# A vision tower on one core: experts 2 to 7 computed on sorted tiles of 128 slots, and the attention stage before them rearranged

## The chip, the cores and the metric

The kernel runs on one core of a Trainium2 chip. The time is that of the device, in microseconds (us); before the change it is 227.14, the median of three runs (226.74 to 228.03). One execution was profiled, and its trace is what is read here.

## The reference

64 images give 36 patches each; a patch embedding, a window attention and a pooled attention with a class row make five rows of 256 numbers per image, and `cls_tok` is put in front, so that there are 6 tokens of 256 for each of 64 images. What follows is an attention over the 6 tokens with a residual, and a mixture of eight experts with a residual:

```python
h = jnp.concatenate([jnp.broadcast_to(cls_tok, (h.shape[0], 1, h.shape[2])), h], axis=1)
h = h + _L0_attn_ref(_layernorm(h, axis=-1), ...)          # 16 heads, causal, ALiBi
h = h + _L0_ffn_ref(_layernorm(h, axis=-1), ...)
# _L0_ffn_ref: E = 8 experts, D = 256, F = 512, two of them for each token
router_probs = jax.nn.softmax(x_flat @ gate_w, axis=-1)
top_k_probs, top_k_idx = jax.lax.top_k(router_probs, TOP_K)      # TOP_K = 2
top_k_probs = top_k_probs / jnp.sum(top_k_probs, axis=-1, keepdims=True)
gate_up = jnp.einsum('nd,edh->enh', x_flat, gate_up_w)
hidden = jax.nn.silu(gate_up[..., :F]) * gate_up[..., F:]
expert_out = jnp.einsum('enf,efd->end', hidden, down_w)
output = jnp.sum(sel * top_k_probs[:, :, None], axis=1)          # sel: the two chosen experts' rows
```

Token 0 is the same for every image up to here (causal attention lets it see only itself), so only 5 x 64 + 1 = 321 rows differ.

## The kernel before, in words

All five engines run instruction streams written out by hand, and every dependence is a counted semaphore; nothing is scheduled by a tool. The order in the source is the order on the engine.

Precision: a product of two fp32 matrices that matters for the routing is made from float32r halves. A tile has a high part (`HI`, a cast, on ScalarE) and a low part (`LO`, the tile minus its high part, on VectorE or GpSimd), and three matmuls (`PRODUCTS`) are summed. So all weights of `gate_up` and `down` pass through `weights_hi` and `weights_lo` before they are used. Other matmuls are plain fp32; the profile has two MATMUL records for each of those.

The stages, in the order of time:

1. The patch convolution (L419, L434), turns (L443), keys and values of the window attention (L496), up to 78.5 us. VectorE makes the scores and weights of the window attention beside it.
2. From 78.5 to 129.5 us: the weighted values are summed by TensorE (`tail_agg`, L539: 18 matmuls against the identity for each of two row tiles), projected (`tail_proj`), added to the window means on VectorE (`local_out`), normalised and turned (`tail_pool`), the pooled scores of the class row (L686), its softmax, and then the projections and softmax of the attention over 6 tokens in three blocks (`att_scores`, `att_weights`), the weighted values (L357 on GpSimd and VectorE), their turns (L634), the output projection (L643), three layer norms (`mid`) and the router (L657). `keep_clock` (L664) are matmuls whose result nobody reads.
3. From 129.5 us: the experts. Every expert is applied to all 322 columns (`NCOL`) of the turned rows `ms`. `gate_up(q, n)` (L744) makes one of four chunks of 128 hidden units, gate in one bank and up in another, with 12 matmuls of 322 columns (two halves, two pieces of the 256 inputs, three products); ScalarE applies Silu, VectorE multiplies, and both split the result into `hids`. `down(s, e)` (L757) makes three banks of 128 rows, 12 matmuls each, and `accumulate` (L1523) adds them to `acc` with the router's weight, which is zero for the experts not chosen. Two experts' weights (1536 KB each) are held in `raw`, loaded by SP, and the next pair's are loaded as the splits of these are done.
4. The rows are stored by SP and ScalarE's queue; the class row goes from one partition of `acc` to its 64 places.

## Time and profile before

| | |
|---|---|
| median of three runs | 227.14 us |
| the profiled execution's own time | 228.78 us |
| its span in the trace | 227.0 us |
| TensorE, matmuls | 207.6 us busy, 1368 records |
| VectorE | 155.6 us busy, 363 |
| ScalarE | 101.6 us busy, 225 |
| GpSimd | 79.5 us busy, 91 |
| mean granted TensorE clock | 0.985 |
| moved by DMA | 23.01 MB, 101 GB/s over the span |

PE is TensorE, PEld its weight loads, DVE VectorE, ACT ScalarE, POOL GpSimd, SP the engine that issues DMAs; SPq is SP's queue. A timeline row gives the start, the length, engine, line, operation, tiles and count of merged records, and in brackets the idle time before it and who ended it. The length of a merged row holds the last record's way through the array too, so the pace is read from the start of one row to the start of the next.

### The profile page before, as it was taken

Reading aid. Unit: us, or ns where it says so; the run is one execution under the profiler, and the core shown is the slowest. Engines: PE = TensorE matmul, PEld = TensorE weight load, DVE = VectorE, ACT = ScalarE, POOL = GpSimd, SP = SyncE. Lnnn points to the kernel's source line nnn. Section 1 sums busy time; section 2 is a strip of 40 time slices with the busy share of each in tenths; the row PEclk is TensorE's granted clock in tenths of the full one; section 3 lists DMA queues with packets and bytes.
Section 4 is the critical chain, followed back from the end, with each engine's and each line's share of the span. In section 5 each row is a group of like instructions: output and inputs, shape, how many; then the busy total and the mean of one; then the engine's idle time right before and its main releaser. Section 6 shows DMA issues by size and latency. Waiting matters only on the chain.

```text
span 227.0 us, 4002 instructions
## 1 busy us (share of the span) xinstructions
PE 207.6 (91%) x1368; PEld 192.4 (85%) x1368; DVE 155.6 (69%) x363; ACT 101.6 (45%) x225; POOL 79.5 (35%) x91
## 2 busy tenths in 40 slices
PE   2999989999999988789587989999999999999983
PEld 2898969898987878477386889999999999999983
DVE  2565981929696767577987599576957785858541
ACT  3754581835354516334122177383718371717030
POOL 0037093555428302270643315233423332333200
PEclk9999999999999999969889999999999999999999
DMA  6999910002910000000000005172533253400004
GB/s 222 360 394 373 339 52 3 3 0 54 423 80 1 3 0 0 0 3 0 1 0 0 3 0 206 76 277 53 225 128 149 43 234 97 180 0 3 0 0 69
DMA packets 4890, 23.01 MB, mean 101 GB/s; under 512 B 694, under 2 KB 2444, under 8 KB 3724
## 3 DMA queue, kind: packets, MB, share of 16 engines
q1 hardware_dynamic: 3960, 21.26, 26.3%
q10 hardware_dynamic: 916, 1.58, 2.0%
q8 instruction: 8, 0.13, 0.2%
q14 instruction: 6, 0.05, 0.1%
HBM read 22.44 MB, written 0.39 MB: 101 GB/s over the span
## 4 chain that ended last, share of the span: by engine, by line
PE 82%; DVE 8%; ACT 3%; DMA 2%; issue 2%; POOL 0%; SPq 0%; DVEq 0%
PE bank L744 26%; PE bank L757 15%; PE bank L419 11%; PE bank L496 9%; PE bank L539 4%; PE bank L434 3%; DMA raw<-conv_w 2%; PE bank L443 2%; PE bank L634 2%; PE bank L618 2%; PE bank L643 1%; PE bank L476 1%; DVE stats L1162 1%; PE bank L657 1%; PE bank L694 1%
## 5 line engine op out<-in xcount | busy, mean ns | idle before, releaser
L744 PE MATMUL bank<-split 128*128 128x322 f32 x384 | 59.2, 314 | 0.6 <-DVE vprod L1531 0.6
L744 PEld LDWEIGHTS bank<-split 128*128 128x128 f32 x384 | 57.6, 188 | 0.9 <-issue 0.9
L1147 POOL TENSOR_TENSOR split<-raw,split 128x256 fp32r<-128x256 f32 x32 | 29.0, 906 | 56.7 <-DVE split L1484 56.7
L757 PE MATMUL bank<-split 128*128 128x256 f32 x288 | 36.0, 283 | 0.6 <-DVE split L1537 0.6
L757 PEld LDWEIGHTS bank<-split 128*128 128x128 f32 x288 | 35.4, 192 | 0.8 <-DVE split L1537 0.8
L419 PE MATMUL bank<-split 128*128 128x256 f32 (+1 forms) x225 | 28.2, 284 | 1.0 <-DVE split L1259 1.0
L419 PEld LDWEIGHTS bank<-split 128*128 128x128 f32 (+1 forms) x225 | 27.5, 191 | 1.5 <-DVE split L1259 1.4
L1044 POOL TENSOR_TENSOR rstd<-veps,mhalf 128x1 f32<-128x1 f32 (+2 forms) x17 | 14.2, 838 | 38.5 <-DVE veps L1169 38.4
L496 PE MATMUL bank<-split 128*128 128x512 f32 x108 | 26.9, 399 | 0.0
L1011 ACT ACTIVATE vprod<-bank 128x322 f32<-128x322 f32 x32 | 13.9, 436 | 24.8 <-PE bank L744 24.7
L1531 DVE TENSOR_TENSOR vprod<-bank,vprod 128x322 f32<-128x322 f32 x32 | 15.7, 491 | 12.0 <-PE bank L744 8.5
L496 PEld LDWEIGHTS bank<-split 128*128 128x128 f32 x108 | 19.8, 188 | 3.9
L1479 DVE TENSOR_TENSOR split<-raw,split 128x512 fp32r<-128x512 f32 x29 | 20.7, 712 | 2.3 <-ACT split L881 2.2
L1019 ACT CAST split<-vprod 128x322 fp32r<-128x322 f32 x32 | 14.8, 463 | 16.4 <-DVE vprod L1531 16.3
L881 ACT CAST split<-raw 128x512 fp32r<-128x512 f32 x32 | 19.5, 613 | 2.5 <-DMA raw<-ffn_w 2.5
L1523 DVE SCALAR_TENSOR_TENSOR pe_rows<-bank,wgt,pe_rows 128x256 f32<-128x256 f32 x24 | 11.2, 479 | 11.1 <-PE bank L757 11.1
L1162 DVE BATCH_NORM_STATS2 stats<-pe_rows 128x6 f32<-128x256 f32 x24 | 9.0, 418 | 12.5 <-ACT pe_rows L794 12.3
L1058 POOL TENSOR_TENSOR window<-window,pe_rows 128x256 f32<-128x256 f32 x14 | 13.7, 982 | 9.0 <-ACT pe_rows L794 8.4
L1537 DVE TENSOR_TENSOR split<-vprod,split 128x322 fp32r<-128x322 f32 x32 | 15.9, 497 | 1.4 <-ACT split L1019 1.4
L855 ACT ACTIVATE kv_rows<-bank,rstd 128x512 f32<-128x512 f32 x18 | 12.0, 690 | 8.5 <-PE bank L496 8.5
L794 ACT COPY pe_rows<-bank 128x256 f32<-128x256 f32 x18 | 6.5, 374 | 18.7 <-PE bank L419 17.0
L434 PE MATMUL bank<-split 128*128 128x256 f32 (+1 forms) x45 | 9.1, 385 | 5.1 <-ACT split L808 5.1
(161 smaller groups left out, 276.2 us busy)
## 6 DMA issues: line engine op xcount, KB each, us to landing
raw<-ffn_w SPq DMA_DIRECT2D x8, 1536.0 KB, 6.5
raw<-xa SPq DMA_DIRECT2D x5, 768.0 KB
tok<-tok_w SPq DMA_DIRECT2D x1, 1536.0 KB, 12.4
tok<-tok_w SPq DMA_DIRECT2D x1, 776.0 KB, 6.4
raw<-xa ACTq DMA_DIRECT2D x1, 576.0 KB, 5.1
raw<-xb SPq DMA_DIRECT2D x6, 96.0 KB
att<-att_w SPq DMA_DIRECT2D x1, 488.0 KB, 13.9
raw<-conv_w SPq DMA_DIRECT2D x1, 384.0 KB, 5.7
```

Of the source, the lines that this page charges most:

```text
L419: mm = pe.matmul(bank[b][:, 0:C], xs[0:n, g % 2, px, a:a + P], cws[0:n, pw, k, :], start=(k == 0 and m == 0), stop=(k == len(KCH) - 1 and ...
L434: mm = pe.matmul(bank[j][:, 0:C], xs[0:n, 0, px, a:a + P], cws[0:n, pw, k, :], start=(k == 0 and m == 0), stop=(k == len(KCH) - 1 and m == 2))
L496: mm = pe.matmul(bank[b][:, :], lns[:, g % 2, px, a:a + P], wkvs[:, pw, aw:aw + 2 * C], start=(c == 0 and m == 0), stop=(c == CC - 1 and m ...
L744: mm = pe.matmul(bank[b][:, 0:NCOL], aws[:, q, pw, a:a + P], ms[:, px, c, FIRST:ROWS], start=(c == 0 and m == 0), stop=(c == CC - 1 and m ...
L757: mm = pe.matmul(bank[b][:, 0:C], hids[:, px, s * FQ + q, a:a + P], bws[:, s, pw, q * C:(q + 1) * C], start=(q == 0 and m == 0), stop=(q = ...
L881: act.copy(aws[:, q, HI, :], a_raw[:, slot, q, :]).then_inc(a_hi, 1)
L1019: act.copy(hids[:, HI, s * FQ + q, FIRST:ROWS], hidf[:, q % 2, :]).then_inc(hid_hi, 1)
L1044: pool.tensor_tensor(rstd[0:parts, k, 0:n], veps[0:parts, k, 0:n], mhalf[0:parts, 0:n], ALU.pow).then_inc(rstd_done, 1)
L1147: pool.tensor_tensor(bws[:, s, LO, q * C:(q + 1) * C], b_raw[:, s, q, :], bws[:, s, HI, q * C:(q + 1) * C].bitcast(F32), ALU.subtract).the ...
L1479: dve.tensor_tensor(aws[:, q, LO, :], a_raw[:, slot, q, :], aws[:, q, HI, :].bitcast(F32), ALU.subtract).then_inc(a_split, 1)
L1531: dve.tensor_tensor(hidf[:, q % 2, :], bank[5 + q % 2][:, 0:NCOL], sg[:, q % 2, :], ALU.mult).then_inc(hid_done, 1)
L1537: dve.tensor_tensor(hids[:, LO, s * FQ + q, FIRST:ROWS], hidf[:, q % 2, :], hids[:, HI, s * FQ + q, FIRST:ROWS].bitcast(F32), ALU.subtract ...
```

## The change

It has two parts. Both are in the diff, which is cut to its core.

**Experts.** Experts 0 and 1 (`DENSE`) stay as they were. For experts 2 to 7 the rows that chose one are counted and given slots, each expert from a multiple of 128 on; with 321 rows, 2 picks and 6 experts that needs at most 10 tiles of 128 slots (`SLOT_TILES`), and 10 are always computed. VectorE works out the slots (steps 11 to 29 of `route_step`), GpSimd scatters each row with its number and its weight to `expert_rows` in DRAM with six indirect DMAs, whose unused slots were filled with zeros long before, from `zero_row`, by SP. SP reads the expert of each tile into a register (`value_load`) and loads its weights into rings of three (`a_ring`, `b_ring`), and the rows of a tile into one of four row buffers (`xr`). For a tile, TensorE turns the rows, makes gate and up as 12 matmuls of 512 columns with the rows as the stationary operand, turns the product, makes the down product as 4 plain fp32 matmuls and puts the result back to its rows with 6 matmuls against a 0/1 matrix `back`, which GpSimd makes; these sums stand in three banks over all ten tiles. Expert 1's down products come at the end (`late_down`), and three VectorE additions close the sums.

**Before the experts.** The window attention's weighted values are summed partly on VectorE and GpSimd; the biases and residuals go through TensorE into the same bank; the pooled rows are no longer normalised and turned a second time, their norm is folded into the weights (`gwvc`, `uc`) and scores; the class row's softmax runs on 128 partitions instead of 8; two of the three layer norms in each set are applied by ScalarE straight from the bank; the second attention block's products move from GpSimd to VectorE, and blocks are taken in the order 0, 2, 1.

```diff
+DENSE = 2
+SPARSE = E - DENSE
+SLOT_TILES = (PICKS * NTOK - SPARSE) // P + SPARSE
+RING = 3
+ROW_RING = 4
...
+            sp.wait_ge(zero_ready, 1)
+            sp.dma_start(expert_rows[0:SLOTS, :].rearrange("(s p) n -> p s n", p=P), spread(zero_row[:, :], 1, SLOT_TILES)).then_inc(zeroed, 16)
...
-            with sp.Fori(1, E // 2) as pair:
...
+            sp.wait_ge(route_step, ROUTED)
+            expert = [sp.value_load(tile_expert[0:1, s:s + 1], min_val=DENSE, max_val=E - 1) for s in range(RING)]
+            tile_a(0, expert[0])
+            tile_b(0, expert[0])
+            tile_a(1, expert[1])
+            expert += [sp.value_load(tile_expert[0:1, s:s + 1], min_val=DENSE, max_val=E - 1) for s in range(RING, SLOT_TILES)]
+            sp.wait_ge(scattered, PICKS * RT * 16)
+            for s in range(ROW_RING):
+                tile_rows(sp, s)
...
+            def class_values_mean():
+                wait_free(pe, 7, "gwv_mean")
+                pe.wait_ge(tok_rest_in, 16)
+                for m in range(CC):
+                    for c in range(CC):
+                        pe.matmul(bank[7][:, C + m:C + m + 1], gwv[:, c, m * P:(m + 1) * P], w_tok("gkv_b")[:, c:c + 1], ...)
+                pe.wait_ge(gwv_scaled, 1)
+                for c in range(CC):
+                    mm = pe.matmul(bank[7][:, 0:C], mean_w[:, :], gwvc[:, c, :], start=(c == 0), stop=(c == CC - 1))
...
+            def second_aggregate():
...
+                for n in (*range(GT), *range(2 * GT, NW)):
+                    if n % GT == 0:
+                        pe.wait_ge(vprod_step, VSTEPS + (4 if n else 3))
+                    for c in range(CC):
+                        mm = pe.matmul(bank[c][:, 0:P], vprod[:, n, c * P:(c + 1) * P], ident, start=(n == 0), stop=(n == NW - 1))
...
+            def tile_gate_up(s):
+                pe.wait_ge(rows_split, s + 1)
+                for half in range(2):
...
+                    for c in range(CC):
+                        piece = half * CC + c
+                        pe.wait_ge(tile_a_split, FQ * s + piece + 1)
+                        for m, (px, pw) in enumerate(PRODUCTS):
+                            mm = pe.matmul(bank[half][:, :], xst[:, s % 2, px, c * P:(c + 1) * P], aws[:, piece, pw, :], ...)
+                        mm.then_inc(tile_a_used, 1)
...
+            for s in range(SLOT_TILES):
+                tile_gate_up(s)
+                if s + 1 < SLOT_TILES:
+                    rows_turn(s + 1)
+                if s:
+                    tile_out(s - 1)
+                if s > 1:
+                    give_back(s - 2)
+                if s + 1 == SLOT_TILES:
+                    late_down(2)
+                hidden_turn(s)
+            give_back(SLOT_TILES - 2)
+            late_down(0)
+            tile_out(SLOT_TILES - 1)
+            late_down(1)
+            give_back(SLOT_TILES - 1)
...
+            for j in range(RT):
+                for i in range(PICKS):
+                    scatter(i, j)
+            way_back(0)
+            for q in range(FQ):
+                down_lo(1, q)
...
+            for s in range(SLOT_TILES):
+                if s + 1 < SLOT_TILES:
+                    tile_weights_lo(s + 1, 0)
+                tile_product(s)
+                if s + 1 < SLOT_TILES:
+                    rows_lo(s + 1)
+                    for piece in range(1, FQ):
+                        tile_weights_lo(s + 1, piece)
+                if s:
+                    out_lo(s - 1)
...
+            for i, (j, _) in enumerate(OUT_BANKS):
+                dve.wait_ge(sums_full, i + 1)
+                dve.wait_ge(acc_done, 2 * RT + i + 1)
+                dve.tensor_tensor(acc[:, j, :], acc[:, j, :], bank[SUM_BANK[j]][:, 0:C], ALU.add).then_inc(result_done, 1)
```

TensorE's experts before, one expert of the loop, its last chunk of `gate_up` and its `down` (L744 is `gate_up`, L757 `down`):

```order
L744 MATMUL bank<-split 128x322 x12
L751 ISA
L757 MATMUL bank<-split 128x256 x12
L751 REGISTER_ALU
L757 MATMUL bank<-split 128x256 x12
L751 REGISTER_ALU
L757 MATMUL bank<-split 128x256 x12
```

TensorE now, from expert 0 on and through the first three tiles (L954 dense `gate_up`, L964 dense `down`, L977 the counts, L986 `rows_turn`, L1001 `tile_gate_up`, L1010 `hidden_turn`, L1019 `tile_out`, L1031 `give_back`):

```order
L977 MATMUL bank<-mask,ones 128x6
L954 MATMUL bank<-split 128x322 x60
L964 MATMUL bank<-split 128x256 x36
L954 MATMUL bank<-split 128x322 x24
L986 MATMUL bank<-con,window 128x128 x2
L1001 MATMUL bank<-split 128x512 x12
L986 MATMUL bank<-con,window 128x128 x2
L1010 MATMUL bank<-con,kv_rows 128x128 x4
L1001 MATMUL bank<-split 128x512 x12
L986 MATMUL bank<-con,window 128x128 x2
L1019 MATMUL bank<-kv_rows,loT 128x256 x4
L1010 MATMUL bank<-con,kv_rows 128x128 x4
```

The tile loop has taken the place of six of eight experts; expert 1's `down` is no longer behind its `gate_up`.

VectorE now, in the routing (L1998 is `hidden`, the product of a dense chunk, L2061 the low part of expert 1's weights, L2003 the low part of the hidden rows, the others slot arithmetic):

```order
L2041 TENSOR_TENSOR pick_eq<-pick_eq,swgt 128x18
L2043 TENSOR_REDUCE pe_rows<-pick_eq 128x3
L2045 TENSOR_TENSOR pe_rows<-swsum,pe_rows 128x3
L1998 TENSOR_TENSOR vprod<-bank,vprod 128x322
L2047 TENSOR_TENSOR kv_rows<-tile_no,first_tile 128x60
L2049 TENSOR_REDUCE tile_sum<-kv_rows 128x10
L2051 TENSOR_SCALAR tile_expert<-tile_sum 128x10
L2061 TENSOR_TENSOR split<-raw,split 128x512
L1998 TENSOR_TENSOR vprod<-bank,vprod 128x322
```

Before, the router's steps stood together ahead of the first product; now they stand between the products of expert 0, and the first low part of expert 1's weights is behind all of them.

SP now, from the last of the first three register loads to the rows of the first tiles (`window` holds `xr`, `kv_rows` and `raw` the rings); of the seven loads at L521 the last is shown:

```order
L517 TENSOR_LOAD tile_expert
L517 ISA x2
L507 ISA
L507 DMA kv_rows<-ffn_w 128x2048
L513 ISA
L513 DMA kv_rows<-ffn_w 128x1024
L507 ISA
L507 DMA raw<-ffn_w 128x2048
...
L521 TENSOR_LOAD tile_expert
L521 ISA x2
L429 DMA window<-expert_rows 128x258 x4
```

The rows of tile 0 are the fourth thing SP does after the routing, behind ten register loads and three weight loads.

## Rows read from the trace of the kernel before

**Rows 1.** The page: busy time by engine, and the chain by line.
```profile
PE 207.6 (91%) x1368; PEld 192.4 (85%) x1368; DVE 155.6 (69%) x363; ACT 101.6 (45%) x225; POOL 79.5 (35%) x91
...
PE bank L744 26%; PE bank L757 15%; PE bank L419 11%; PE bank L496 9%; PE bank L539 4%; PE bank L434 3%; DMA raw<-conv_w 2%; PE bank L443 2%; PE bank L634 2%; PE bank L618 2%; PE bank L643 1%; PE bank L476 1%; DVE stats L1162 1%; PE bank L657 1%; PE bank L694 1%
```

**Rows 2.** Windows: stretch, length, busy and count by engine, clock, DMA share, GB/s.
```profile
78.50:96.00 17.50, 14.85 (x104) 12.80 (x103) 10.73 (x26) 6.79 (x21) 2.67 (x5) 1.00 0.00 0
96.00:113.00 17.00, 13.43 (x51) 9.97 (x50) 13.90 (x30) 5.10 (x17) 8.65 (x11) 0.86 0.01 1
...
133.90:222.00 88.10, 87.44 (x637) 87.27 (x638) 62.38 (x144) 42.94 (x93) 27.50 (x30) 1.00 0.29 108
```

**Rows 3.** Timeline of PE, the experts: start, length, what, idle before.
```profile
141.22 4.48 PE L757 MATMUL bank<-split 128*128 128x256 f32 x36
145.54 7.36 PE L744 MATMUL bank<-split 128*128 128x322 f32 x48
152.73 4.48 PE L757 MATMUL bank<-split 128*128 128x256 f32 x36
...
220.01 3.49 PE L757 MATMUL bank<-split 128*128 128x256 f32 x27 [0.61 <-DVE split L1537]
```

**Rows 4.** Timeline of PE, earlier stages.
```profile
22.05 0.82 PE L443 MATMUL bank<-con,pe_rows 128*128 128x128 f32 x6
22.62 5.63 PE L419 MATMUL bank<-split 128*128 128x256 f32 x45
...
28.67 4.34 PE L496 MATMUL bank<-split 128*128 128x512 f32 x18
33.97 5.64 PE L419 MATMUL bank<-split 128*128 128x256 f32 x45 [0.97 <-DVE split L1259]
...
101.40 1.89 PE L694 MATMUL bank<-poolT,tok 128*128 128x256 f32 x8
```

**Rows 5.** Groups by line and shape: busy us, mean ns, idle before.
```profile
L1479 DVE TENSOR_TENSOR split<-raw,split 128x512 fp32r<-128x512 f32 x29 | 20.7, 712 | 2.3 <-ACT split L881 2.2
...
L881 ACT CAST split<-raw 128x512 fp32r<-128x512 f32 x32 | 19.5, 613 | 2.5 <-DMA raw<-ffn_w 2.5
...
L855 ACT ACTIVATE kv_rows<-bank,rstd 128x512 f32<-128x512 f32 x18 | 12.0, 690 | 8.5 <-PE bank L496 8.5
...
L1523 DVE SCALAR_TENSOR_TENSOR pe_rows<-bank,wgt,pe_rows 128x256 f32<-128x256 f32 x24 | 11.2, 479 | 11.1 <-PE bank L757 11.1
...
L1408 DVE TENSOR_TENSOR split<-bank,split 128x256 fp32r<-128x256 f32 x3 | 1.3, 421 | 1.2 <-ACT split L968 1.2
...
L1440 DVE TENSOR_TENSOR kv_rows<-bank,kv_rows 128x512 f32<-128x512 f32 x1 | 0.7, 693 | 1.2 <-PE bank L702 1.2
```

**Rows 6.** Timeline: marks of the attention stage and of the routing.
```profile
85.53 4.26 PE L539 MATMUL bank<-con,vprod 128*128 128x128 f32 x36 [0.24 <-DVE vprod L348]
...
95.48 1.03 PE L686 MATMUL bank<-poolT,u 128*8 128x256 f32 x4 [0.90 <-ACT poolT L798]
...
110.69 0.23 DVE L1387 TENSOR_TENSOR kv_rows<-kv_rows,r 128x72 f32<-128x72 f32 x1
...
129.65 0.18 DVE L1488 COPY lg<-bank 128x24 f32<-128x24 f32 x1 [0.92 <-PE bank L657]
...
133.21 0.18 DVE L1515 TENSOR_TENSOR wgt<-rtop,rrec 128x24 f32<-128x24 f32 x1
```

**Rows 7.** Timeline: GpSimd and VectorE at the same time.
```profile
107.35 1.54 POOL L366 TENSOR_TENSOR vprod<-kv_rows 128x640 f32<-128x640 f32 x1 [5.25 <-ACT kv_rows L951]
...
107.44 1.53 DVE L1374 TENSOR_TENSOR kv_rows<-kv_rows,m 128x72 f32<-128x72 f32 x1
```

**Rows 8.** The DMA view: GB/s by slice of 5.7 us; issues, KB each, us to landing.
```profile
GB/s 222 360 394 373 339 52 3 3 0 54 423 80 1 3 0 0 0 3 0 1 0 0 3 0 206 76 277 53 225 128 149 43 234 97 180 0 3 0 0 69
...
raw<-ffn_w SPq DMA_DIRECT2D x8, 1536.0 KB, 6.5
...
out<-pe_rows ACTq DMA_DIRECT2D x3, 64.0 KB, 2.8
```

More of the change, by code:

```diff
@@ L700, in _ @@
[L700 to L708 removed]
+            second_aggregate()
+            local_rows(1)
@@ L1010, in chunk @@
                 act.wait_ge(gate_ready, n + 1)
-                act.activation(sg[:, q % 2, :], bank[q % 2][:, 0:NCOL], ACT.Silu).then_inc(silu_done, 1)
-                if not (last and s == 1 and q + AHEAD_A >= FQ):
-                    nxt = q + AHEAD_A >= FQ
-                    slot = (s + nxt) % 2
-                    loads = 16 * (pair + 1 + (s + nxt) // 2)
-                    weights_hi(slot, (q + AHEAD_A) % FQ, loads if (q + AHEAD_A) % FQ == 0 else None)
-                act.wait_ge(hid_done, n + 1)
@@ L1019, in chunk @@
-                act.copy(hids[:, HI, s * FQ + q, FIRST:ROWS], hidf[:, q % 2, :]).then_inc(hid_hi, 1)
-            with act.Fori(0, E // 2 - 1) as pair:
-                for s in range(2):
-                    for q in range(FQ):
-                        chunk(2 * pair + s, s, q, pair, False)
-            for s in range(2):
-                for q in range(FQ):
-                    chunk(E - 2 + s, s, q, E // 2 - 1, True)
+                if n >= 2:
+                    act.wait_ge(hid_done, n - 1)
@@ new lines, in scatter, with way_back @@
+            def scatter(i, j):
+                pool.indirect_dma_start(expert_rows, bass.IndirectOffsetOnAxis(ap=dest_row[:, i, j:j + 1], axis=0),
+                                        xrow[:, j, i, :], None).then_inc(scattered, 16)
+            def way_back(s):
+                wait_tile_in(pool, rows_in, s)
+                pool.wait_ge(*((given, s - 1) if s >= 2 else (down_done, RT)))
+                pool.tensor_scalar(back[:, s % 2, :], token_row[:, :], xr[:, s % ROW_RING, ROW_TOKEN:ROW_TOKEN + 1], None,
+                                   ALU.is_equal).then_inc(back_done, 1)
@@ L1540, in expert_pair @@
-            def expert_pair(pair, last):
-                for s in range(2):
-                    e = 2 * pair + s
-                    for q in range(2, FQ):
-                        chunk(e, s, q, pair, last)
-                    if not (last and s == 1):
-                        for q in range(2):
-                            chunk(e + 1, 1 - s, q, pair + s, last)
-                    accumulate(e)
-            chunk(0, 0, 0, 0, False)
-            chunk(0, 0, 1, 0, False)
-            with dve.Fori(0, E // 2 - 1) as pair:
-                expert_pair(pair, False)
```

1250 lines of the change are left out of this document (842 added, 408 removed).

## The prediction

> **What bounds the kernel now.** First the page's busy line and the chain by line: TensorE is busy 207.6 of 227.0 us, and the two expert lines L744 and L757 make 41% of the chain, more than any other pair [rows 1]. Then the windows: from 133.9 to 222.0 TensorE is busy 87.4 of 88.1 us at full clock while VectorE has 62 and ScalarE 43, so the experts cost what their matmuls cost. From 78.5 to 113 it is different: TensorE idles 2.7 and 3.6 us, the clock granted from 96 to 113 falls to 0.86, and VectorE is as busy as TensorE, 13.9 of 17.0 us [rows 2]. There a chain through all engines decides. So the change is priced twice: by matmuls in the experts, by the chain before them. I measure both from one mark, the copy of the router's logits on VectorE: 129.65 [rows 6]. Behind it lie 227.0 - 129.65 = 97.4 us.
>
> **Paces of TensorE.** From starts of merged rows: a split matmul of 322 columns takes (152.73 - 145.54)/48 = 0.150 us, of 256 columns (145.54 - 141.22)/36 = 0.120 [rows 3]; of 512 columns 4.34/18 = 0.241; a turn of 128x128 (22.62 - 22.05)/6 = 0.095; four plain fp32 matmuls of 256 columns 1.89 [rows 4].
>
> **Experts, the work.** Six dense experts go: each 48 x 0.150 + 36 x 0.120 = 11.5 us, together 69. A tile costs 12 x 0.241 = 2.89 for gate and up, 2 x 0.095 = 0.19 to turn the rows, 1.89 for down, 6 x 0.120 = 0.72 to give back, 4 x 0.095 = 0.38 to turn the product: 6.07, ten tiles 60.7. The counts add about 0.5. On TensorE alone the change is worth 69 - 61.2 = 7.8 us. A sparse count does not show in it, since ten tiles are always run.
>
> **Experts, is a tile TensorE's?** VectorE has per tile four low parts at 0.71, a product of 512 columns 0.69, the rows' low part 0.42 and the output's 0.48: 4.4 us. ScalarE has four high parts at 0.61 and four others of at most 0.69: 5.2 [rows 5]. Both are under 6.07. In order: with t from the start of gate and up, its four pieces are used at 0.7, 1.4, 2.2, 2.9. ScalarE refills them at 1.4, 2.8, 4.2, 4.8, its Silu lying between the first two and the rows' high part before the third. VectorE makes the product by 3.7 and the last low part by about 6.2, against a need at 8.2 (6.07 + 3 x 0.72). The turn of the product, at 5.7, finds it ready since 3.7. Each hand-over has 2 us to spare, so the period is TensorE's. Weights: 1.57 MB and 0.13 MB of rows per tile are 280 GB/s at this period; slices of the trace show 394 and 423 [rows 8]. Each load is issued more than one period ahead. I cost DMA at nothing; its cover is that distance.
>
> **Experts, the start**, in us after the mark. TensorE does the first chunk to 1.8, counts to 2.6, and three more chunks to 8.0. VectorE's router steps go at 0.2 to 0.35 each; before, the twelve took from 129.65 to 133.4 [rows 6]. Now 23 more stand between the first products. At about 0.21 each and 0.49 per product, the slots are out at 7.5, the tile numbers at 8.6 and the first low part of expert 1's weights at 9.3. The fifth chunk waits for that: 1.3 us idle. Then chunks to 12.9, expert 0's down (36 x 0.12 = 4.3) to 17.2, two chunks to 20.8, the turn of the first rows to 21.0, and their high and low parts (0.37 and 0.42, with hand-overs): tile 0 starts at 22.0. Tiles 0 and 1 are uneven, since ScalarE must also cast four pieces of expert 1's down weights in tile 0, and its delay reaches down product, Silu and the next rows; by the same bookkeeping tile 2 starts at 31.8. Seven periods later it is 74.3. The last tile, without a row turn and with one late down group of 12 x 0.12 = 1.44, takes 7.3. The tail is 0.72 + 1.44 + 1.89 + 1.44 + 0.72 = 6.2. Last matmul: 87.8. From the last matmul to the end the trace has 227.0 - 223.5 = 3.5 us [rows 3], and the last step, one VectorE operation on 256 columns and a store, is of the same kind. That gives 91.3, against 97.4: **6.1 us gained**.
>
> **What the start hides.** Six indirect scatters, a read-back, and ten register loads are in no row. One scatter costs GpSimd no less than a short queue entry and no more than the 2.8 us a 64 KB store takes from issue to landing [rows 8]; I take 1.1, nearer to the GpSimd operations of its size, so issue ends at 14.2 and data has landed at 16.5. A register load lies between 0 and 2.8 too; I take 0.7, so SP has its three at 10.7, the three weight loads out at 12, the other seven at 17. Rows then land at about 20, against a need at 20.8. If both cost next to nothing nothing is won, since the chunks cover them. At the upper end of either, SP or GpSimd is done 12 to 15 us later. I add 0.5 for this. The zeros are issued right behind the last patch load, in the first quarter of the span, long before the scatters wait for them.
>
> **The stage before.** It starts worse. `class_values_mean` puts four one-column and two plain matmuls, 1.75 us, where TensorE stood idle for 0.97 [rows 4]: +0.8. VectorE gains two value products and two sums there and delays the class keys by 0.5. The second aggregate, which ran 85.5 to 89.8 as 18 matmuls [rows 6], starts at 86.0 behind a VectorE sum and has 12: it ends at 88.9. From there a chain is shortened link by link. The projection lands on its bias, and the copied rows are ready at 90.7 against 92.1. The pooled norm's apply, its turn and two affine copies are gone, so the pooled scores come at 91.5 against 95.5. The softmax of the class row and the projections behind it keep this lead, and the block-0 weights are done at 106.4 against 110.9 [rows 6]. Then GpSimd's three value products, a turn, the projection, and for the last row tile a context turn of 9 matmuls at 114.3, the projection at 117.9, statistics at 118.8, GpSimd's root behind three splits and two copies at 120.3, the norm, turn and split, and the router. The logits come at 123.6 instead of 129.65: **6.0 us gained**, by durations of rows 4 and 5. No row shows `negative_mean`; I take 0.3 to 0.5 for it, in the chain once.
>
> Where VectorE and GpSimd meet, the trace has this: a VectorE operation on 72 columns took 1.53 us, exactly beside a GpSimd operation of 1.54 [rows 7]. By the Trainium skill (SBUF — State Buffer, Who interferes with whom) a VectorE instruction with two SBUF inputs and a GpSimd one that reads SBUF take turns at a shared port, and the second blocks until the first ends; the trace agrees. By that rule, `way_back` blocks VectorE once in a tile, for up to its 0.7 us or so, and 4.4 becomes 5.1, which still changes nothing; in the routing it speaks against the change, and is part of a rival.
>
> **The sum.** 228.8 - 6.1 - 6.0 + 0.5 = 217.2 for an execution under the profiler. The median of the runs shown is 227.14 where this one took 228.8, so 1.6 less: 215.6. I round to 216, since two hand-overs per stage will be longer than booked.
>
> **Rivals.**
> 1. *The tiles wait for their rows.* Scatters or register loads at 1.5 to 2.5 us, or VectorE's four low parts and GpSimd's scatters held up by each other as in rows 7, move tile 0 by 2 to 6 us. For it: all of this stands in one line from the slots at 7.5 to the need at 20.8, with under 1 us to spare. Against it: 12 us of chunks lie over it. 216 + 2 to 6 = 218 to 222.
> 2. *The stage before gains little.* VectorE and GpSimd were busy there, products were moved to VectorE, and ScalarE gets the norms. Each link may give back half: +3 to +5, so 219 to 221.
> 3. *Slower: the tile loop is paced by something else.* If weights come as the eight loads did, 6.5 us for 1536 KB, one at a time, a tile of 1.7 MB takes 7.2 us, and the loop 10 us more: 226. It turns to slower from 7.3 us a tile, (227 - 216)/10 above 6.07 + 0.1. At 8 us, with scattered rows and weights in each other's way, it is 234. Against it: the loads overlap, and the slices at 394 and 423 GB/s need 4 us per tile.
> 4. *More is gained.* The clock no longer falls to 0.86, and TensorE's idle time there shrinks: 212 to 214.
>
> **Chances.** Forecast 214 to 218: 0.5. Rival 1: 0.22. Rival 2: 0.12. Rival 3: 0.06, of which 0.04 slower. Rival 4: 0.1. About 0.5%, 1.1 us, is what a measurement of this kernel tells from no change. Faster 0.94, same 0.02, slower 0.04. The range leaves out the far half of rival 1 and all of rival 3: 212.5 to 221.5.
>
> **What would show it.** Right: `tile_gate_up` rows of 12 matmuls starting 6.0 to 6.2 us apart from tile 2 on; the logits' copy at 122.5 to 125; the first tile 21 to 23 us after it; TensorE idle once for about 1 us before the fifth chunk. Wrong: VectorE or ScalarE busy over 90% in the tile loop with TensorE idle in each period (rival 3 in another form), TensorE waiting for a DMA of `expert_rows` before the first tile (rival 1), or the logits later than 126 (rival 2).

## The result and the profile after

The changed kernel takes 225.86 us (median of 20 runs, 224.51 to 229.19) beside 227.24 us before in the same series (226.19 to 229.47): a ratio of 0.9923, 95% interval 0.9896 to 0.9951. It is faster, by 0.8% and not by the 5% that were forecast; 225.86 lies 4.4 us above the upper end of the range. The profiled execution took 225.82 us, its span is 224.0 us. Here and below, medians and spreads are of all executions, while ratios leave out the few, of either kernel, that took over 1.5% longer than the fastest of the same kernel.

First the page of the kernel after, three lines of it: busy time, the clock by slice of 5.6 us, the chain by line.

```profile
PE 199.7 (89%) x1190; PEld 175.0 (78%) x1190; DVE 145.1 (65%) x338; ACT 114.4 (51%) x247; POOL 79.3 (35%) x103
...
PEclk9999999999999999999999999976999999999999
...
PE bank L1001 12%; PE bank L552 10%; PE bank L1019 7%; PE bank L629 6%; DMA window<-expert_rows 5%; DMA expert_rows<-pe_rows,dest_row 3%; PE bank L1031 3%; POOL expert_rows L1545 2%; DMA raw<-xb 2%; PE bank L853 2%; PE bank L964 2%; PE bank L1010 2%; DVE stats L1621 2%; DVE split L1738 2%; PE bank L862 2%
```

TensorE is busy 7.9 us less than in [rows 1], yet the span is only 3.0 us shorter; and the execution profiled before was 1.6 us above its median, where this one is at its own, so the medians are only 1.4 us apart. What is new on the chain are two transfers of `expert_rows` and GpSimd's scatters, 10% of it together; what is new in the clock are two slices at 0.7 and 0.6, from 145.6 to 156.8 us. The windows of [rows 2], after:

```profile
78.50:96.00 17.50, 15.90 (x89) 12.56 (x87) 13.09 (x38) 7.93 (x24) 7.14 (x9) 1.00 0.00 1
96.00:113.00 17.00, 13.68 (x72) 11.49 (x73) 13.23 (x36) 7.29 (x25) 6.53 (x12) 1.00 0.01 1
```

The clock does not fall between 96 and 113 in this execution (0.86 before). In the second profile of the same kernel, after_again below, it is 0.96 from 78 us to the mark. The mark, the copy of the router's logits, is at 125.07 where [rows 6] have 129.65: the stage before gained 4.6 us. But 98.9 us lie behind the mark, where there were 97.4: **the sorted tiles and the tail lost 1.5 us**. The timeline of TensorE in the kernel after, from the last two dense chunks to tile 3:

```profile
141.51 3.76 PE L954 MATMUL bank<-split 128*128 128x322 f32 x24
149.40 0.69 PE L986 MATMUL bank<-con,window 128*128 128x128 f32 x2 [4.14 <-DMA window<-expert_rows]
151.01 2.50 PE L1001 MATMUL bank<-split 128*128 128x512 f32 x5 [0.92 <-DVE split L2073]
...
157.07 3.23 PE L1001 MATMUL bank<-split 128*128 128x512 f32 x12
160.35 1.89 PE L1019 MATMUL bank<-kv_rows,loT 128*128 128x256 f32 x8
162.44 3.02 PE L1001 MATMUL bank<-split 128*128 128x512 f32 x12
...
168.30 3.01 PE L1001 MATMUL bank<-split 128*128 128x512 f32 x12
```

and the chain of waits of the same stretch, start and length:

```profile
132.72 1.22 POOL expert_rows L1545
...
139.74 7.47 DMA expert_rows<-pe_rows,dest_row
147.22 0.02 issue
147.24 2.12 DMA window<-expert_rows
...
151.01 4.80 PE bank L1001 x12
```

To be seen: TensorE stands still for 4.14 us until the read-back of the rows (`window<-expert_rows`) has come, and the read-back waited for the last scatter. That one was issued at 139.74, its GpSimd instruction was over at 140.9, and its data counted as landed at 147.2, 6.3 us later. Then the first tile's 12 matmuls take 4.80 us where later ones start the next group after 2.9. The window from 145 to 157, with columns as in [rows 2]:

```profile
145.00:157.00 12.00, 6.31 (x21) 4.42 (x20) 4.17 (x10) 4.18 (x10) 1.26 (x1) 0.72 0.71 249
```

TensorE had been idle for over 4 us, and the clock granted is 0.72 on the mean: some of these matmuls run at the lower of the two levels (1.2 and not 2.4 GHz). Last the end, all engines of the kernel after:

```profile
217.16 0.88 PE L1031 MATMUL bank<-split 128*128 128x256 f32 x6
...
217.76 1.07 DVE L2129 TENSOR_TENSOR pe_rows<-pe_rows,bank 128x256 f32<-128x256 f32 x3
218.20 0.64 SPq L535 DMA_DIRECT2D out<-pe_rows  x1
218.53 3.01 ACTq L437 DMA_DIRECT2D out<-pe_rows  x3
```

The last matmul ends at 218.04, the kernel 6.0 us later; before it was 3.5. L535 is the store of the class row from one partition to its 64 places. It is issued 5.8 us before the end. In the kernel before, the timeline of SP has it 5.75 us before the end (227.0), but 2.3 us before the last matmul was over:

```profile
221.25 0.62 SPq L402 DMA_DIRECT2D out<-pe_rows  x1
```

### The profile page after: what moved, and what is told of

It reads as the page before. It is cut to its first block, busy times and chain, and to the rows that moved or that the text cites. A ratio compares the mean times of both kernels' runs of the same rounds, so it can differ in the third digit from the quotient of the medians.

```text
span 224.0 us, 3577 instructions
## 1 busy us (share of the span) xinstructions
PE 199.7 (89%) x1190; PEld 175.0 (78%) x1190; DVE 145.1 (65%) x338; ACT 114.4 (51%) x247; POOL 79.3 (35%) x103
## 4 chain that ended last, share of the span: by engine, by line
PE 55%; DVE 18%; DMA 10%; issue 5%; POOL 3%; ACT 3%; SPq 2%; ACTq 0%; DVEq 0%
PE bank L1001 12%; PE bank L552 10%; PE bank L1019 7%; PE bank L629 6%; DMA window<-expert_rows 5%; DMA expert_rows<-pe_rows,dest_row 3%; PE bank L1031 3%; POOL expert_rows L1545 2%; DMA raw<-xb 2%; PE bank L853 2%; PE bank L964 2%; PE bank L1010 2%; DVE stats L1621 2%; DVE split L1738 2%; PE bank L862 2%
## 5 line engine op out<-in xcount | busy, mean ns | idle before, releaser
L1001 PE MATMUL bank<-split 128*128 128x512 f32 x120 | 32.1, 418 | 0.9 <-DVE split L2073 0.9
L1552 POOL TENSOR_SCALAR split<-token_row,window 128x384 fp32r<-128x384 f32 x10 | 13.4, 1344 | 46.2 <-PE bank L1031 37.7
L1001 PEld LDWEIGHTS bank<-split 128*128 128x128 f32 x120 | 23.0, 200 | 6.4 <-DVE split L2073 1.3
L552 PEld LDWEIGHTS bank<-split 128*128 128x128 f32 (+1 forms) x225 | 27.6, 191 | 0.4 <-DVE split L1740 0.2
L629 PE MATMUL bank<-split 128*128 128x512 f32 x108 | 26.4, 397 | 0.0
L1471 POOL TENSOR_TENSOR rstd<-veps,mhalf 128x1 f32<-128x1 f32 (+2 forms) x17 | 14.2, 838 | 25.9 <-DVE veps L1628 25.7
L629 PEld LDWEIGHTS bank<-split 128*128 128x128 f32 x108 | 19.8, 188 | 3.9
L954 PE MATMUL bank<-split 128*128 128x322 f32 x96 | 15.3, 316 | 0.3 <-DVE split L2061 0.3
L1371 ACT CAST split<-raw 128x512 fp32r<-128x512 f32 x24 | 14.3, 621 | 2.1 <-PE bank L1001 2.1
L954 PEld LDWEIGHTS bank<-split 128*128 128x128 f32 x96 | 14.4, 188 | 0.6 <-DVE split L2061 0.6
L2082 DVE TENSOR_TENSOR kv_rows<-bank,kv_rows 128x512 f32<-128x512 f32 x10 | 6.9, 692 | 9.5 <-PE bank L1001 6.9
L567 PEld LDWEIGHTS bank<-split 128*128 128x128 f32 (+1 forms) x45 | 8.2, 277 | 5.4 <-ACT split L1099 5.4
L2066 DVE TENSOR_TENSOR split<-kv_rows,split 128x512 fp32r<-128x512 f32 x16 | 10.4, 686 | 2.6 <-ACT split L1371 2.5
L1738 DVE TENSOR_TENSOR split<-raw,split 128x1536 fp32r<-128x1536 f32 x5 | 8.8, 1754 | 4.7 <-ACT split L1108 4.7
L1371 ACT CAST split<-kv_rows 128x512 fp32r<-128x512 f32 x16 | 9.5, 620 | 2.0 <-DMA kv_rows<-ffn_w 1.1
```

What stands on the lines that cost most here:

```text
L552: mm = pe.matmul(bank[b][:, 0:C], xs[0:n, g % 2, px, a:a + P], cws[0:n, pw, k, :], start=(k == 0 and m == 0), stop=(k == len(KCH) - 1 and ...
L567: mm = pe.matmul(bank[j][:, 0:C], xs[0:n, 0, px, a:a + P], cws[0:n, pw, k, :], start=(k == 0 and m == 0), stop=(k == len(KCH) - 1 and m == 2))
L629: mm = pe.matmul(bank[b][:, :], lns[:, g % 2, px, a:a + P], wkvs[:, pw, aw:aw + 2 * C], start=(c == 0 and m == 0), stop=(c == CC - 1 and m ...
L954: mm = pe.matmul(bank[b][:, 0:NCOL], aws[:, q, pw, a:a + P], ms[:, px, c, FIRST:ROWS], start=(c == 0 and m == 0), stop=(c == CC - 1 and m ...
L1001: mm = pe.matmul(bank[half][:, :], xst[:, s % 2, px, c * P:(c + 1) * P], aws[:, piece, pw, :], start=(c == 0 and m == 0), stop=(c == CC - ...
L1371: act.copy(aws[:, piece, HI, :].rearrange("p (q n) -> p q n", q=FQ), a_ring[ring(s)][:, :, piece * P:(piece + 1) * P]).then_inc(tile_a_hi, 1)
```

## Experiments

Each version ran four to six times, after_again twelve times. Theory A, after this reading: four terms of the forecast were too small, each at its own place. (1) The scatters' data lands late because the weights of the first tiles, 2.5 MB, are on the same DMA engines. (2) The pause lets the clock fall, which stretches tiles 0 and 1. (3) The class row's store, not the last matmul, sets the end. (4) In the stage before, something in the class row's chain. The rivals are in the expectations. Ratios are to the kernel before, run on the same chip.

**rows_first: the weights behind the rows.**

```diff
             tile_a(0, expert[0])
-            tile_b(0, expert[0])
-            tile_a(1, expert[1])
...
             for s in range(ROW_RING):
                 tile_rows(sp, s)
+            tile_a(1, expert[1])
+            tile_b(0, expert[0])
             tile_b(1, expert[1])
```

> SyncE issues only tile 0's gate-and-up weights before it waits for the scattered rows; the weights of tile 1 and the down weights of tiles 0 and 1 are issued behind the four row loads. Theory A (the scatters' data lands 6.3 us after the last scatter because 2.6 MB of weights are on the same DMA engines): it lands in 2.3 to 3 us, the row turn starts 3 to 3.5 us earlier, at about 146, and tile 0 starts with it; tile 1's weights are then about 1 us late, so the kernel takes 223 us. Rival B (6.3 us is the scatter's own): the row turn stays at 149, the weights come later still, and the kernel takes 226 to 228 us.

224.29 us (223.11 to 225.88), ratio 0.9885 (0.9808 to 0.9962). The timeline of SP, then of TensorE:

```profile
144.20 1.76 SPq L429 DMA_DIRECT2D window<-expert_rows  x4
...
146.28 0.44 PE L986 MATMUL bank<-con,window 128*128 128x128 f32 x2 [0.58 <-DMA window<-expert_rows]
147.64 3.07 PE L1001 MATMUL bank<-split 128*128 128x512 f32 x12 [0.92 <-DVE split L2073]
...
154.42 0.66 PE L1010 MATMUL bank<-con,kv_rows 128*128 128x128 f32 x4 [3.49 <-DVE kv_rows L2082]
154.84 4.59 PE L1001 MATMUL bank<-split 128*128 128x512 f32 x12
```

The last scatter's instruction ended at 141.36, so its data landed in 2.8 us, not 6.3, and TensorE waits 0.58 us for the rows, not 4.14. Theory A (1) holds. The price was larger than I wrote: the weights of tile 1, issued at 146.15, took 6.25 us, and TensorE waits 3.49 us in tile 0. The pause has moved, and the slow stretch with it: tile 0's 12 matmuls take 3.07 us, and it is now tile 1's, behind the pause, that take 4.59 (mean clock 0.79 from 152 to 160). That the total fell at all can't be told from the changed kernel by these intervals; the wait's two places can.

**no_scatter: the whole of the start.**

```diff
-            for j in range(RT):
-                for i in range(PICKS):
-                    scatter(i, j)
...
-            sp.wait_ge(scattered, PICKS * RT * 16)
+            sp.wait_ge(zeroed, 16)
```

> The six scatters are left out (the tiles then compute on zeros, so the output lacks experts 2 to 7); SyncE reads the rows back once the zeros and its ten register loads are done. Theory A (what was mis-sized at the start is the way of the rows, and the cold clock that follows from it): TensorE is idle under 1 us before tile 0, tile 0 starts 22 us after the copy of the logits, tile 2 at 32, and the kernel takes 220 to 221 us. Rival (VectorE's and ScalarE's order, or the register loads, would have held tile 0 up anyway): tile 2 starts 35 us or more after the mark, and the kernel takes 223 us or more.

220.96 us (219.87 to 222.68), ratio 0.9751 (0.9680 to 0.9822). Its mark is at 125.10:

```profile
145.86 0.44 PE L986 MATMUL bank<-con,window 128*128 128x128 f32 x2 [0.59 <-DMA window<-expert_rows]
147.22 3.02 PE L1001 MATMUL bank<-split 128*128 128x512 f32 x12 [0.92 <-DVE split L2070]
...
156.89 2.99 PE L1001 MATMUL bank<-split 128*128 128x512 f32 x12
```

Tile 0 starts 22.1 and tile 2 31.8 us after the mark, and the last matmul ends 86.9 after it. The forecast had 22.0, 31.8 and 87.8. So the rest of its start (routing, chunks, splits, register loads) adds up right; what failed in it is the way of the rows. Two smaller errors cancel in that sum: before the fifth chunk TensorE waits 0.3 us and not 1.3, and before the turn of the rows it waits 0.6 where nothing was booked.

**keep_clock: the pause filled with matmuls that nobody reads.**

```diff
             gate_up(3, FQ + 3)
+            pe.wait_ge(route_step, PLACED)
+            keep_clock(3, 8)
             rows_turn(0)
```

> Eight fp32 matmuls on 256 columns, whose result nobody reads, fill 3.8 of the 4.1 us for which TensorE waits for the rows; nothing else moves. If the low granted clock behind the pause is what stretches tile 0 (4.8 us of gate and up in place of 2.9), tile 0 takes 2.9 us and tile 2 starts 1.6 us earlier: 224.2 us. Rival (tile 0 is stretched by ScalarE's and VectorE's pieces, which come late for the same reason as the rows): tile 0 stays at 4 us or more and the kernel at 225.5 to 226 us.

224.45 us (223.61 to 227.69), ratio 0.9868 (0.9788 to 0.9948). The timeline of TensorE, and the window from 145 to 157:

```profile
151.42 3.04 PE L1001 MATMUL bank<-split 128*128 128x512 f32 x12 [0.92 <-DVE split L2075]
155.73 3.23 PE L1001 MATMUL bank<-split 128*128 128x512 f32 x12
161.10 3.02 PE L1001 MATMUL bank<-split 128*128 128x512 f32 x12
```

```profile
145.00:157.00 12.00, 9.86 (x49) 7.83 (x49) 6.26 (x13) 6.05 (x15) 1.74 (x2) 1.00 0.71 256
```

The idle time is filled but for 0.59 us. The clock is 1.00, tile 0 takes 3.04 us in place of 4.80, and tile 2 starts 9.7 us behind tile 0 in place of 11.4. So the fall costs 1.7 us, as (2) says. The rows come no sooner: tile 0 starts 25.6 us after the mark (125.82).

**early_down: the pause filled with work that is needed.** Two of expert 1's three down groups go before tile 0.

```diff
             gate_up(3, FQ + 3)
+            for i, (j, b) in enumerate(OUT_BANKS[:2]):
+                pe.wait_ge(acc_done, RT + i + 1)
+                down(1, j, b)
             rows_turn(0)
...
-                if s + 1 == SLOT_TILES:
-                    late_down(2)
...
-            late_down(0)
```

ScalarE's `down_hi(1, q)`, GpSimd's `down_lo(1, q)` and VectorE's `accumulate(1, 2)`, `accumulate(1, 0)` and `hidden_lo(7)` move with them, ahead of the rows.

> Two of the three late down groups of expert 1 (12 matmuls each, 1.44 us) move from behind the last tiles into the pause before tile 0; the down weights' high parts go to ScalarE's pauses at 135 to 140 us, their low parts on GpSimd ahead of the first way_back, and the last hidden chunk is split before the rows. Theory A (the pause and the cold clock are real costs that useful work can fill): 2.9 us less at the end and 1.6 us less in tiles 0 and 1: 221.5 us. Rival (the two groups run into the row turn, or the last tiles need them as cover for their hand-overs): 1.5 to 2.5 us less in all: 223.5 us.

220.80 us (219.99 to 221.71), ratio 0.9726 (0.9674 to 0.9778); the expectation of theory A was 221.5.

```profile
146.68 0.62 PE L964 MATMUL bank<-split 128*128 128x256 f32 x3 [0.36 <-DVE split L2002]
148.11 2.05 PE L964 MATMUL bank<-split 128*128 128x256 f32 x15 [0.81 <-DVE split L2002]
149.99 0.38 PE L986 MATMUL bank<-con,window 128*128 128x128 f32 x2
151.30 3.02 PE L1001 MATMUL bank<-split 128*128 128x512 f32 x12 [0.92 <-DVE split L2072]
```

The turn of the rows waits for nothing now, and tile 0 starts as late after the mark as in the changed kernel (25.9 us) with 2.9 us of work less behind it. What TensorE still waits for, 0.36 and 0.81 us, are the low parts of the last hidden chunk. The clock stays at 1.00. The last matmul ends 87.1 us after the mark (93.0 in the changed kernel).

**front_only: one part alone**, the new stage before with all eight experts dense, by the code of the kernel before.

```diff
-            for s in range(SLOT_TILES):
-                tile_gate_up(s)
...
+            with pe.Fori(0, E // 2 - 1) as pair:
+                expert_pair(pair, False)
+            expert_pair(E // 2 - 1, True)
```

> The new stage before with the eight dense experts of the kernel before. Theory A (the parts add, and the sorted tiles lose what they should have gained): the logits' copy comes at 125.1, as in the changed kernel, and 97.4 us follow as before: a span of 222.5 us and 224.3 us in all, 1.5 us less than the whole change. Rival B (the sorted tiles do gain on the same start, or the dense experts run longer behind the new stage): 226 us or more.

225.12 us (222.96 to 225.98), ratio 0.9878 (0.9823 to 0.9933). In the profiled execution the mark is at 124.64 and the span 221.2, so 96.6 us lie behind the mark. The timeline of TensorE and of the class row's store:

```profile
214.22 3.50 PE L940 MATMUL bank<-split 128*128 128x256 f32 x27 [0.61 <-DVE split L1837]
...
215.46 0.61 SPq L508 DMA_DIRECT2D out<-pe_rows  x1
```

The store is issued 2.3 us before the last matmul's end and 5.7 before the kernel's. By the traces theory A holds: the sorted tiles, as the change has them, cost 2.3 us behind the mark instead of gaining. But the execution profiled was the fastest of six, 2.2 us below their median, at a clock of 1.00 throughout, and the median lies between the two expectations. By the runs the intervals of the two ratios, 0.9878 and 0.9923, overlap; that the half beats the whole is likely, not shown.

**no_class_store and class_rows: what sets the end.** The first leaves the class row's store out, so its output lacks that row. The second makes the class row's sums in 64 partitions:

```diff
-            table(token_row[:, :], [[1, ROWS]], 0, 0)
+            table(token_row[:, 0:2 * P], [[1, 2 * P]], 0, 0)
+            pool.memset(token_row[:, 2 * P:2 * P + B], float(2 * P + B - 1)).then_inc(tables_done, 1)
+            table(token_row[:, 2 * P + B:], [[1, P - B]], 2 * P + B, 0)
...
+                act.copy(hids[:, n // FQ, HI * FQ + n % FQ, 0:FIRST], spread(hidf[:, n % FQ, 1], 1, FIRST))
...
-            sp.dma_start(out[:, 0, :].unsqueeze(0), spread(acc[B - 1:B, 2, :], 1, B)).then_inc(out_done, 16)
+            sp.dma_start(out[:, 0, :], acc[0:B, 2, :]).then_inc(out_done, 16)
```

(and the low part likewise, on VectorE).

> The store of the class row to its 64 places is left out, nothing else. Theory A (this store sets the end, since its sum now comes with the other sums): the last matmul is followed by 4.3 to 4.6 us in place of 6.0, 224.3 us. Rival B (the other stores, issued 0.3 to 0.7 us later, end at the same time): 5.7 us or more, 225.7 us.

> The class row's sums are made in 64 partitions instead of one: the 62 unused columns of the dense chunks get a copy of the class column (one more ScalarE and one more VectorE operation on 62 columns a chunk), the table of token numbers repeats the class row's number, and the store reads 64 partitions, one place each. Theory A (the store from one partition is the slow one): as without that store, 224.3 us. Rival B (the store is no slower than others, or 16 small operations cost as much in the dense chunks): 225.7 us or more.

Without the store: 224.67 us (222.43 to 227.37), ratio 0.9862 (0.9781 to 0.9942), and 4.15 us from the last matmul's end (216.35) to that of the span (220.5). With 64 partitions: 223.88 us (223.07 to 224.84), ratio 0.9823 (0.9772 to 0.9874), its end:

```profile
217.65 0.88 PE L1031 MATMUL bank<-split 128*128 128x256 f32 x6
...
218.69 0.52 SPq L535 DMA_DIRECT2D out<-pe_rows  x1
219.02 1.82 ACTq L437 DMA_DIRECT2D out<-pe_rows  x3
```

218.53 to 222.7 are 4.2 us. Both ways 1.8 us are gone, so what is slow is the reading of one partition for 64 places, not the 64 KB; why, no run shows. It slows its neighbours too: by the DMA view the 64 KB stores at the end land 3.6 to 3.7 us after their issue in the changed kernel (medians), and 2.0 to 2.1 us after it in these two. Theory A (3) holds. That the total of class_rows fell by more than 1.8 us is within the intervals.

**combo, combo_class, combo_turn.** combo is early_down with expert 0's third down group behind the last dense chunk, each of the first two weight loads issued as soon as its own register is loaded, and tile 0's down weights behind the rows; VectorE works out the tile numbers ahead of the third chunk's product (`hidden(2)`, not shown here):

```diff
-            for i, (j, b) in enumerate(OUT_BANKS):
+            for i, (j, b) in enumerate(OUT_BANKS[:2]):
                 pe.wait_ge(acc_done, i + 1)
                 down(0, j, b)
             gate_up(2, FQ + 2)
             gate_up(3, FQ + 3)
+            pe.wait_ge(acc_done, 3)
+            down(0, *OUT_BANKS[2])
...
+            for s in range(SLOT_TILES):
+                expert.append(sp.value_load(...))
+                if s < 2:
+                    tile_a(s, expert[s])
```

combo_class adds class_rows; combo_turn adds to that the row turn between the two early groups (`down(1, *OUT_BANKS[0])`, `rows_turn(0)`, `down(1, *OUT_BANKS[1])`).

> As early_down, with three more moves: expert 0's third down group goes behind the last dense chunk, so that the last chunk's split (TensorE waited 1.2 us for it) is covered; SyncE issues each of the first two weight loads as soon as its own tile number is loaded, and tile 0's down weights behind the rows; the tile numbers are worked out ahead of the third product. Theory A (the rows then land 1 us earlier, in time, with 0.5 MB fewer weights on the engines): tile 0 starts 1.2 to 1.4 us earlier than in early_down, 219.4 us. Rival B (the rows still end last, or tile 1 then waits for its weights): 220.5 us or more.

> combo and class_rows together. Theory: the two gains are in different places and add: the end 4.2 us behind the last matmul (6.0 in combo), 1.8 us less than combo: a ratio to before of 0.960 where combo had 0.968. Rival: the 16 small operations on 62 columns, harmless in class_rows where TensorE had a pause behind them, now delay the last chunks, since the pause is filled: half of the gain or less, 0.964 or more.

> combo_class with the turn of tile 0's rows put between the two early down groups of expert 1, so that the rows' high and low parts are made beside the second group. Theory (TensorE's wait of 0.9 us for that split is a cost in itself): tile 0 starts 0.9 us earlier, 0.9 us less in all. Rival (the rows land at about the same time as the turn is now asked for, so that TensorE waits for them, and the second group has only moved behind that wait): no gain, 0.2 us either way.

combo: 221.01 us (219.23 to 222.84), ratio 0.9677 (0.9619 to 0.9736); tile 0 starts 25.0 us after its mark, 0.9 earlier than in early_down where theory A had 1.2 to 1.4, and the read-back is issued 3.6 us after the last scatter's instruction, with 2 MB of weights before it. By the totals combo can't be told from early_down: the intervals of the ratios overlap. combo_class: 222.19 us (219.47 to 223.66), ratio 0.9754 (0.9701 to 0.9807), no better than combo. Its early groups:

```profile
147.00 0.63 PE L965 MATMUL bank<-split 128*128 128x256 f32 x3 [1.08 <-DVE split L2008]
148.70 2.06 PE L965 MATMUL bank<-split 128*128 128x256 f32 x15 [1.07 <-DVE split L2008]
```

Line 2008 is the hidden chunks' low part, late by the added operations on 62 columns: 2.15 us of waiting where combo has 0.6. Here the rival was right: what was harmless behind a pause is on the path once the pause is full. In the two profiled executions the end is 1.8 us shorter than in combo, and yet 92.7 us lie behind the mark where combo has 92.6. combo_turn: 220.14 us (219.74 to 221.03), ratio 0.9662 (0.9617 to 0.9706); it waits 2.5 us at the same operation, its turn waits for no row, and tile 0 starts 26.1 us after the mark where combo_class has 26.9: 0.8 of the 0.9 us expected.

**after_again: the changed kernel beside them.**

> The changed kernel as it is, beside the others on the same chip, to compare the versions with it directly: 225.9 us, and again about 4 us of TensorE's time before tile 0 spent waiting for the read-back, with the last scatter's data landing about 6 us after its issue, if that wait is of this kernel and not of the one execution profiled.

226.45 us (224.98 to 229.01, 12 runs), ratio 0.9909 (0.9875 to 0.9942). TensorE waits 4.11 us for the read-back, and the last scatter lands 6.45 us after its instruction: the wait belongs to the kernel.

**tables_early: the stage before.** The trace of the kernel after shows in the class row's chain, for GpSimd, VectorE and TensorE:

```profile
92.41 3.73 POOL L1529 TENSOR_TENSOR split<-raw,split 128x512 fp32r<-128x512 f32 x3
...
92.42 1.34 DVE L1731 SCALAR_TENSOR_TENSOR bound<-con,bound 128x64 f32<-128x64 f32 x1
...
97.02 1.10 PE L759 MATMUL bank<-both_halves,kv_rows 128*128 128x64 f32 x8 [1.11 <-DVE kv_rows L1931]
```

L1731 belongs to the tables of the routing, of no use there; it works on 64 columns and takes 1.34 us, about as long as one of GpSimd's three beside it (1.24 on the mean).

```diff
-            local_moments(1)
             tables()
+            local_moments(1)
```

> VectorE's seven table operations (the bounds for the router's ties, the counting table) go from behind the second statistics of the local stage, where they stand in the chain of the class row and the last of them took 1.34 us beside a GpSimd operation, to ahead of those statistics, where VectorE was idle for 1.7 us. Theory A (the stage before fell short of the forecast by this place): TensorE's wait of 1.1 us before the class row's aggregate goes, the logits' copy comes 1.2 to 1.5 us earlier against the start of the second aggregate (37.7 us behind it in place of 39.1), and the kernel takes 1.3 us less, 224.6 us beside 225.9. Rival B (the chain then waits for GpSimd's roots and the exponentials, which are as late): under 0.4 us less.

224.84 us (223.43 to 226.67), ratio 0.9850 (0.9784 to 0.9917).

```profile
91.05 0.22 DVE L1731 SCALAR_TENSOR_TENSOR bound<-con,bound 128x64 f32<-128x64 f32 x1
...
96.61 1.10 PE L759 MATMUL bank<-both_halves,kv_rows 128*128 128x64 f32 x8
```

The same operation takes 0.22 us, with GpSimd idle beside it, TensorE's wait is gone, and from the start of the second aggregate to the mark there are 38.0 us in place of 39.1. By the total alone it can't be told from the changed kernel (the intervals overlap); the stretch can: it is 39.1 us in the traces of rows_first, keep_clock, early_down and front_only too. Theory A holds for 1.1 of the 1.45 us that the stage before lacked; where the other 0.35 went stays open.

**best: the gains together**, combo with the row turn between the early groups and the tables early, without class_rows.

> combo, with the turn of tile 0's rows between the two early down groups and with the tables early; the class row stored from one partition as in the changed kernel. Theory: three independent gains add, 0.9 us (tile 0's rows are split beside a down group) and 1.3 us (tables) below combo: a ratio to before of 0.958, 218.3 us. Rival (the rows have not landed when the turn is asked for, and the tables' gain is no gain): 0.966 or more, like combo.

218.21 us (216.89 to 219.24), ratio 0.9557 (0.9498 to 0.9615), where 0.958 was expected: the fastest version, 4.4% below the kernel before. Its mark is at 124.41:

```profile
146.70 0.38 PE L987 MATMUL bank<-con,window 128*128 128x128 f32 x2
146.84 1.68 PE L965 MATMUL bank<-split 128*128 128x256 f32 x12
148.35 2.91 PE L1002 MATMUL bank<-split 128*128 128x512 f32 x12
```

The rows are split beside the second early group, and tile 0 follows without a gap, 23.9 us after the mark.

## Why the prediction was wrong, step by step

The numbers behind the mark are us after it; "after" is the kernel after.

| step | forecast | after |
|---|---|---|
| second aggregate starts, ends | 86.0, 88.9 | 86.0, 88.9 |
| pooled scores | 91.5 | 91.85 |
| the mark | 123.6 | 125.07 |
| issue of the scatters ends | 14.2 | 15.8 |
| their data has landed | 16.5 | 22.2 |
| rows there | 20 | 24.3 |
| tile 0 | 22.0 | 25.9 |
| tile 2 | 31.8 | 37.4 |
| tile 2 to tile 9 | 42.5 | 42.25 |
| last matmul ends | 87.8 | 93.0 |
| end | 91.3 | 98.9 |

**What held.** The stage before to the pooled scores. On TensorE, 7.8 us less work was forecast for the experts; behind the mark it is busy 83.9 us in no_scatter, where hardly any of it runs at the lower clock, beside 92.6 before. The loop's period is TensorE's (6.07 forecast; the last five tiles start 5.86 apart, since from the start of the down product to the next group it is 1.55 us, 165.50 to 167.05 in the trace, and I had taken the merged length of 1.89; one tile waits 0.91 us for its rows), VectorE and ScalarE are no bound, and `way_back`, 1.3 us each and not 0.7, costs nothing. Rival 3 is out. The register loads were out of the way in time: in no_scatter, where nothing else holds the read-back, it is issued 15.2 us after the mark, against the 17 booked.

**What failed, by its size.** In order: the mark 1.45 late, of which 1.1 is the VectorE operation held beside GpSimd (tables_early). The start, 3.9: the step "data has landed at 16.5" took the landing of a lone small store for that of a scatter behind 2.5 MB of weights; it was 6.3 us and not 2.3 (rows_first, no_scatter), and a scatter takes 1.1 us on the mean and 0.30 to the next, not 1.1 in all. Tiles 0 to 2, 1.7: a pause of TensorE was priced at its length, without the lower clock behind it (keep_clock). The end, 2.5: "from the last matmul to the end ... of the same kind" was wrong. Before, the class row's store had 2.3 us of matmuls over it; the change makes all three sums behind the last matmul, so its 5.8 us lie bare (class_rows takes back 1.8). Most of the other 0.7 are the sums themselves: three behind the last matmul take VectorE 1.07 us, where one took 0.48. The tile loop and the last tile with the tail give 0.4 back. 1.45 + 3.9 + 1.7 + 2.5 - 0.4 = 9.1 us on the span, and the allowance of 0.5 for the start was in the sum already: 8.6 us, from 217.2 to 225.8.

From 217.2 the forecast went down to 216, another 1.2 us, and that is a fifth step that failed. It took 1.6 us off, because the execution profiled before stood that far above its median; the one profiled after does not (225.82 beside 225.86). That execution had the clock at 0.86 from 96 to 113 and 0.985 on the mean. The kernel before ran again beside the experiments: 12 executions at a mean clock of 1.00 took 226.0 to 227.3 us, 12 at 0.985 took 228.2 to 229.8 (and one, left out, 230.8). So the excess was most likely the fallen clock in the very stage whose gain was forecast by that execution's marks, and was taken off twice. Where the clock falls in the others no trace shows.

**The rivals.** Rival 1 named the right place, TensorE waiting for a DMA of `expert_rows`, and a price that held for it alone (2 to 6 us; 3.9 + 1.7 came), but as the only thing that goes wrong; 0.22 was little for a chain with under 1 us to spare and two lengths in no row. Rival 2 did not come: the logits' copy is at 125.07, before its 126, though the 1.1 us that VectorE was held by GpSimd are of its kind. Rival 4's condition came true in the execution profiled, the clock from 96 to 113 is 1.00, and gave nothing on top of the 6.0 us forecast for this stage: it is most likely part of the 4.6 that came. The mistake common to three of the four terms in the sum to 8.6: each was priced by a row in which the same thing stood under cover or alone.

I had weighed the rule of the shared port only for the tiles and the routing. The Trainium skill (SBUF — State Buffer, Who interferes with whom) has a VectorE instruction with two SBUF inputs contend with a GpSimd one that reads SBUF, and the order of issue decide which of them waits; the same operation at 1.34 us beside GpSimd and 0.22 apart from it agrees, and it was the stage before where this was on the path. For the landing: the Trainium skill (DMA: Bandwidth & Descriptors, Queues, rings and completion order) has each DMA engine take turns between queues, a packet at a time. The runs show that more queued weights mean a later landing: 2.8 us with 1 MB issued before, 3.6 to 4.1 with 2 MB (combo, combo_turn, combo_class, best), 5.2 to 6.5 with 2.5 MB (after and the other six traces of that order). Whether it is by such turns none of them shows.

## What to carry to other kernels

Where a transfer is waited for, price its landing with what its neighbours on the DMA engines have queued, and issue behind it what is needed later. A pause of TensorE of some 4 us costs more than its length; before removing it, look for work that stands uncovered elsewhere and fits in (early_down gained more than either cure of the pause alone). At the end of a kernel, look at when the slowest store is issued, not at the last matmul: moving its data to the last step uncovers it. And where the execution profiled stands off its median, look for the stage in which it does before carrying the difference over: if the change touches that stage, the difference may go with it.

## What the hardware showed

- A scatter of 128 rows of 1032 bytes held GpSimd for 0.96 to 1.36 us (once, in class_rows, for 3.05), with 0.30 to the next; the data landed 2.8 us after the last one with 1 MB of loads issued before, 3.6 to 4.1 us with 2 MB, 5.2 to 6.5 us with 2.5 MB.
- After 4.1 us of idle TensorE the mean clock from 145 to 157 was 0.72; 12 split matmuls of 512 columns took 4.8 us (5.49 in after_again, 4.59 after 3.49 us of idle time in rows_first) in place of 3.0.
- A store of 1 KB from one partition to 64 places was issued 5.7 to 5.8 us before the end in three kernels (before, after, front_only); 64 KB from 64 partitions, issued 0.16 us after the last matmul's end, let the kernel end 4.0 us later.
- A VectorE operation on 64 columns with two SBUF inputs took 0.22 us alone and 1.34 beside a GpSimd operation on 512 columns.
